# A gated delta rule with a triangular solve: a new order of steps, three elements in flight, the solve's turned blocks by transfer

## The chip, the cores and the metric

One core of one Trainium2 chip runs the program. The metric is device time in microseconds, from start to end of one launch. The core has five instruction queues that run beside each other: TensorE (PE), VectorE (DVE), ScalarE (ACT), GpSimd (POOL) and SyncE (SP, here for DMA only). Each runs its instructions in the order written and waits on semaphores where another queue's result is needed.

## The reference, cut to what matters

For each of 32 batch elements x (256 tokens x 128 features) the kernel does an attention-like layer and a small feed-forward layer, and adds both to x:

```
xn = layernorm(x)
q, k, v = silu(causal_conv4(xn @ Wq | Wk | Wv))      # 12 heads, 64 wide for q and k, 128 for v
beta = sigmoid(xn @ Wb + b_b);  g = -exp(A_log) * softplus(xn @ Wgk + dt_bias)
q, k = l2norm(q) * 64**-0.5, l2norm(k)
for each token t, each head:                         # S is 64 x 128
    S  = S * exp(g_t)
    S += k_t (outer) (v_t - k_t S) * beta_t
    o_t = q_t S
attn = (rms_norm(o) * (xn @ Wg) * sigmoid(xn @ Wg)) @ Wo
ffn  = fp4(silu(fp4(xn) @ fp4(w_gate)) * (fp4(xn) @ fp4(w_up))) @ fp4(w_down)
out  = x + attn + ffn
```

fp4(.) rounds blocks of 16 numbers to eight magnitudes. All is fp32.

## The kernel before, in words

The recurrence over tokens is done in two chunks of 128 tokens per head. Inside a chunk the products k_i.k_j with their decays form a triangular 128 x 128 matrix whose inverse is needed; there are 12 heads x 2 chunks = 24 of them per element (NU). Their 32 x 32 diagonal blocks, 4 x 24 = 96, are inverted on POOL, one block in each partition ("lanes"): SP writes the blocks from the tile UP to a DRAM tensor `to_lanes` (step LOUT, four transfers) and loads them as 96 lanes into `laneA` (LLOAD); POOL solves by columns (LANEP, 30 pairs of a product at L568 and a sum at L571, each waiting for the one before by `link`); SP stores them (STORE) and fetches them back onto the diagonals (FETCH, four transfers). The larger blocks of the inverse then come from small matmuls on PE: MY, MZ for 64 x 64 and MY2, MX, MZ2 for 128 x 128. Some of these need diagonal blocks turned; the kernel before turns them on VectorE (MT, L986, three stream transposes for each group of 8 units, read from UP, written to the tile N64).

Work on one element is written as named steps. `ORDER` is a list of (step, index, offset): in iteration `it` the step is done for element it + offset. Each engine walks the same list (`of(it)`) and emits only its own part of each step, so ORDER fixes the order in every queue. A name without r is the product on PE (QK: projection of q and k for a head pair; VP: values; QT, VT, KT, OT, HT: transposes; DD: the decays; GR: k.k and k.q; GC: cumulative gates; GP: gate; WO, YO: output; FU: feed-forward); with r it is the reader on ACT or DVE. QKt and VPt are the taps of the convolution on VectorE (L856), QKs and VPs the silu, QN and SSr the norms, CJ scalars, GRr the masked products into UP (L950), DDg POOL's input of DD (L549), LN and LN2 the layer norm (VectorE, with rstd at L538 on POOL and the load of xin by SP), XQ0 and HQ the fp4 rounding, SE and SO the pipelined slots of the recurrence over heads, SQ, OS and OG output norm and gate (rO at L577 is on POOL). PE's results go to six PSUM banks used as a ring; `ring_plan` works the uses out from ORDER.

In the kernel before all of an element's steps have offset 1 up to the first pieces of the solve and offset 0 after. The loop (`run`) does iterations -1 and 0 straight, then a hardware loop of 15 bodies with two iterations each, then the last one. LN and LN2 of the next element stand near the head of ORDER, behind three of the solve's four pieces (LANEP 0 to 2) and ahead of the last (LANEP 3, offset 0):

```
("VT", 2, 0), ("LN", 0, 1), ("LN2", 0, 1), ("VT", 5, 0), ("VTr", 2, 0), ("XN", 0, 1), ("XNr", 0, 1),
("QK", 0, 1), ("ZB", 0, 1), ("ZBr", 0, 1), ...
("QKt", 0, 1), ("QKr", 1, 1), ("ZBg", 0, 1), ("LANEP", 3, 0), ("DDg", 0, 1), ("STORE", 0, 0), ...
```

Of the kernel before, what the change touches and what calls it, by code (L numbers as in the profile page):

```python
# [11 lines left out]
P = 128  # L12
# [11 lines left out]
PIECES = 4  # L24
# [27 lines left out]
    ("VT", 2, 0), ("LN", 0, 1), ("LN2", 0, 1), ("VT", 5, 0), ("VTr", 2, 0), ("XN", 0, 1), ("XNr", 0, 1),  # L52
    ("QK", 0, 1), ("ZB", 0, 1), ("ZBr", 0, 1), ("QK", 1, 1), ("QKr", 0, 1), ("ZBe", 0, 1), ("QK", 2, 1),
    ("QKt", 0, 1), ("QKr", 1, 1), ("ZBg", 0, 1), ("LANEP", 3, 0), ("DDg", 0, 1), ("STORE", 0, 0), ("QKs", 0, 1),
    ("QK", 3, 1), ("VT", 4, 0), ("QKr", 2, 1), ("VP", 0, 1), ("QKt", 1, 1), ("QKs", 1, 1), ("QKt", 2, 1),
    ("QKr", 3, 1), ("VTr", 5, 0), ("VTr", 4, 0), ("DD", 0, 1), ("FETCH", 0, 0), ("VPr", 0, 1), ("QKs", 2, 1),
    ("QT", 0, 1), ("QTr", 0, 1), ("QKt", 3, 1), ("MT", 0, 0), ("QN", 0, 1), ("QT", 1, 1), ("QTr", 1, 1),
    ("MT", 1, 0), ("QT", 2, 1), ("DDg", 1, 1), ("DD", 1, 1), ("QTr", 2, 1), ("QKs", 3, 1), ("DDr", 0, 1),
    ("GC", 0, 1), ("MY", 0, 0), ("DDg", 2, 1), ("MYr", 0, 0), ("XQ0", 0, 1), ("QN", 1, 1), ("VP", 1, 1),
    ("GCr", 0, 1), ("QK", 4, 1), ("MZ", 0, 0), ("DDr", 1, 1), ("DD", 2, 1), ("QKr", 4, 1), ("MZr", 0, 0),  # L60
    ("DDg", 3, 1), ("DDr", 2, 1), ("MY2", 0, 0), ("MY", 1, 0), ("QKt", 4, 1), ("QT", 3, 1), ("VP", 2, 1),
    ("MYr", 1, 0), ("VPr", 1, 1), ("MY2r", 0, 0), ("VPr", 2, 1), ("QTr", 3, 1), ("MZ", 1, 0), ("MT", 2, 0),
    ("SSr", 0, 1), ("MY", 2, 0), ("MZr", 1, 0), ("DD", 3, 1), ("MYr", 2, 0), ("DDr", 3, 1), ("QN", 2, 1),
    ("MX", 1, 0), ("MZ2r", 0, 0), ("CJ", 0, 1), ("QK", 5, 1), ("SE", 3, 0), ("VPt", 1, 1), ("MY2r", 1, 0),
    ("QKs", 4, 1), ("MZ", 2, 0), ("GR", 0, 1), ("VPt", 2, 1), ("VPt", 0, 1), ("GRr", 0, 1), ("GRr", 1, 1),
    ("QKr", 5, 1), ("DDg", 4, 1), ("SE", 4, 0), ("MZr", 2, 0), ("GR", 1, 1), ("QKt", 5, 1), ("XQ0", 1, 1),
# [3 lines left out]
    ("QN", 5, 1), ("DDr", 4, 1), ("SO", 7, 0), ("GRr", 4, 1), ("DDg", 5, 1), ("SE", 7, 0), ("SSr", 2, 1),  # L70
    ("DD", 5, 1), ("GRr", 5, 1), ("DDr", 5, 1), ("XQ", 0, 1), ("GRr", 6, 1), ("GRr", 7, 1), ("SO", 8, 0),
# [3 lines left out]
    ("FU", 1, 1), ("LLOAD", 0, 1), ("FUr", 0, 1), ("MZ2r", 2, 0), ("FUm", 0, 1), ("FUr", 1, 1), ("SQ", 11, 0),  # L75
# [6 lines left out]
    ("OTr", 0, 0), ("VP", 4, 1), ("VTr", 0, 1), ("VPt", 3, 1), ("SO", 17, 0), ("VPs", 3, 1), ("OT", 1, 0),  # L82
# [35 lines left out]
def ring_plan(steps):  # L118

    uses, free, frees = {}, list(range(NRING)), {}
    count = [[0] * NRING for _ in range(3)]
    for kind, a, off in steps:
        free += frees.pop((kind, a), [])
        if kind not in RING:
            continue
        for j in range(TAKES.get(kind, 1)):
            assert free, (kind, a)  # L130
            b = free.pop(0)
            uses[kind, a, j] = (b, off, count[off][b], count[2][b])
            count[off][b] += 1
            count[2][b] += 1
            frees.setdefault(reader_of(kind, a, j), []).append(b)
    assert not frees
    return uses, count


def build(nc, x, Wq, Wk, Wv, Wg, Wo, conv_q, conv_k, conv_v, Wgk, Wb, b_b, A_log, dt_bias, gnorm,  # L140
# [13 lines left out]
    with ctx:  # L154
# [46 lines left out]
        eGR = sb("eGR", [P, 2, NU])  # L201
# [9 lines left out]
        sq = sb("sq", [P, 4, 2 * NT * 2, DK])  # L211
# [68 lines left out]
        s_xcd = sem("inverses_turned")  # L280
# [73 lines left out]
        def run(eng, iteration):  # L354

            for it in (-1, 0):
                parity[0] = it % 2
                iteration(it)
            with eng.Fori(1, NB - 2, 2) as it:
                for n in range(2):  # L360
                    parity[0] = (1 + n) % 2
                    iteration(it + n)
            parity[0] = (NB - 1) % 2
            iteration(NB - 1)
# [17 lines left out]
        def corner(a):  # L382

            return N64[:, (par() + a) % 2, :, :, :]

# [15 lines left out]
        def stage(k, lag):  # L401
# [13 lines left out]
            for way in ("to_lanes", "from_lanes"))  # L415

# [9 lines left out]
        def _(sp):  # L426
# [24 lines left out]
            def iteration(it):  # L451
                for kind, a, i in of(it):
# [21 lines left out]
                    if kind == "LLOAD":  # L474
                        sp.wait_ge(s_diag, cnt(i, 1, 1) * 16 * NBL)
                        if not zero(i):
                            hold(sp)
                            sp.wait_ge(s_lout, i * 16)
                        sp.dma_start(laneA[0:LANES, :, :].rearrange("l j i -> l (j i)"),
                                     to_lanes.rearrange("q u j i -> (q u) (j i)")).then_inc(s_lin, 16)  # L480
                    if kind == "STORE":
                        sp.wait_ge(s_solved, cnt(i, 1, 1))
                        if not zero(i):
# [4 lines left out]
                                     laneA[0:LANES, :, :].rearrange("l j i -> l (j i)")).then_inc(s_lout, 16)  # L488
                    if kind == "FETCH":
# [9 lines left out]
        def _(pool):  # L499
# [6 lines left out]
            nc.gpsimd.memset(N64[:, :, :, :, :], 0.0)  # L506
# [15 lines left out]
            chain = [0, 0, 0]  # L522

            def iteration(it):
                first_it = isinstance(it, int) and it < 0
                i0, base = (0, 0) if first_it else (it, chain[2])
                if not first_it:
# [7 lines left out]
                for kind, a, i in of(it):  # L535
# [22 lines left out]
                    if kind == "LANEP":  # L558
# [22 lines left out]
            def counted(it):  # L581
# [9 lines left out]
        def _(act):  # L591
            act.wait_ge(s_wload, 16 * 19)
            nc.scalar.activation(negA[:, :], negA[:, :], ACT.Exp).then_inc(s_seta, 1)
            chain = [0, 0, 0]

            def iteration(it):
                first_it = isinstance(it, int) and it < 0
                i0, base = (0, 0) if first_it else (it, chain[2])
                if not first_it:
# [7 lines left out]
                for kind, a, i in of(it):  # L607
# [63 lines left out]
                    if kind == "VT":  # L671
# [3 lines left out]
                        if not zero(i):  # L675
# [678 lines left out]
```

## Time and profile before

| | |
|---|---|
| median of 3 runs | 3294.02 us (3276.98, 3294.02, 3296.87) |
| the profiled execution | 3276.51 us, span 3274.8 us |
| mean granted TensorE clock | 0.937 of full |
| busy: PE, DVE, ACT, POOL | 2721.0, 2617.8, 2193.7, 1549.4 us |
| DMA | 73.30 MB, q1 9.1% of 16 engines' span |

Busy time is the union of an engine's instructions. In the rows below a bracket at the end of a timeline row is the idle time of the engine just before it and what ended it. The clock column is the share of full TensorE clock granted in the stretch. Line numbers are those of the kernel before.

### The profile page before, as it was taken

How to read it: one execution, taken by the hardware profiler on the slowest of the kernel's cores; microseconds unless marked ns; L12 is line 12 of the kernel's file. 1: busy time of each engine (PE TensorE's matmuls, PEld its weight loads, DVE VectorE, ACT ScalarE, POOL GpSimd, SP SyncE). 2: the span in 40 equal slices, each digit the busy share in tenths (PEclk: the TensorE clock that was granted, in tenths of full speed). 3: DMA queues.
4: the chain of work that ended last, by engine and by line, in shares of the span. 5: the costliest groups of instructions: out<-in, count | busy, mean ns of one | idle time of the engine just before them, and what ended most of it. 6: DMA issues, size and time to landing. Idle time of an engine off the chain costs nothing.

```text
span 3274.8 us, 84555 instructions
## 1 busy us (share of the span) xinstructions
PE 2721.0 (83%) x25330; PEld 2140.6 (65%) x25487; DVE 2617.8 (80%) x7460; ACT 2193.7 (67%) x6594; POOL 1549.4 (47%) x2386
## 2 busy tenths in 40 slices
PE   4588888788888888888888888888878888888896
PEld 2467666676666666666677666667666667666675
DVE  6688888788887878878788887878878788787882
ACT  3466766676776667767667676767767677666674
POOL 1455434554435554445554345554355544355541
PEclk8799999899999999999999999999999999999997
DMA  1110010110110100101100101101101101101100
GB/s 48 22 25 18 20 27 14 27 26 17 23 26 16 26 22 17 26 18 23 26 20 19 27 15 26 26 17 23 26 16 26 26 16 23 27 15 27 26 15 14
DMA packets 241563, 73.30 MB, mean 22 GB/s; under 512 B 207408, under 2 KB 234352, under 8 KB 241008
## 3 DMA queue, kind: packets, MB, share of 16 engines
q1 hardware_dynamic: 241008, 66.71, 9.1%
q8 instruction: 250, 4.10, 0.6%
q14 instruction: 305, 2.50, 0.3%
HBM read 37.32 MB, written 29.36 MB: 20 GB/s over the span
## 4 chain that ended last, share of the span: by engine, by line
DVE 33%; POOL 27%; issue 23%; DMA 6%; PE 6%; SPq 2%; POOLq 1%; DVEq 1%; ACT 1%; ACTq 0%
POOL laneA L571 12%; POOL laneT L568 12%; DVE KQ L856 8%; DVE UP L950 8%; DVE vc L856 4%; DVE N L986 3%; DMA laneA<-to_lanes 3%; DMA to_lanes<-UP 3%; PE ring L1127 2%; POOL rO L577 2%; SPq L473 1%; POOLq L533 1%; DVE ssr L919 1%; DVE xn L880 1%; DVE V L1005 1%
## 5 line engine op out<-in xcount | busy, mean ns | idle before, releaser
L571 POOL TENSOR_TENSOR laneA<-laneA,laneT 96x30 f32<-96x30 f32 (+14 forms) x960 | 514.7, 536 | 75.6
L568 POOL TENSOR_TENSOR laneT<-laneA 96x30 f32<-96x30 f32 (+14 forms) x960 | 488.4, 509 | 68.1 <-POOL laneA L571 0.2
L555 POOL TENSOR_TENSOR sqk<-sse,phalf 128x8 f32<-128x8 f32 x96 | 157.3, 1638 | 700.5 <-DVE sse L924 700.5
L856 DVE SCALAR_TENSOR_TENSOR KQ<-ring,ckq,KQ 128x255 f32<-128x255 f32 (+2 forms) x1152 | 462.9, 475 | 14.4 <-DVE nabs L888 7.0
L856 DVE SCALAR_TENSOR_TENSOR vc<-ring,cvv,vc 128x255 f32<-128x255 f32 (+2 forms) x1152 | 460.0, 475 | 1.2
L549 POOL TENSOR_TENSOR gm<-g,mle 128x512 f32<-128x512 f32 x192 | 197.2, 1048 | 361.8 <-DVE UP L950 270.1
L577 POOL TENSOR_TENSOR rO<-ov,mhalf 128x8 f32<-128x8 f32 x96 | 162.2, 1690 | 357.6 <-DVE ov L1016 350.4
L950 DVE SCALAR_TENSOR_TENSOR UP<-ring,cj,gm 128x256 f32<-128x256 f32 x768 | 317.2, 478 | 2.3 <-PE ring L1144 1.2
L1027 DVE SCALAR_TENSOR_TENSOR V<-V,rO,ring 128x128 f32<-128x128 f32 x768 | 214.8, 343 | 121.5 <-POOL rO L577 62.3
L758 ACT ACTIVATE junk<-V 128x128 f32<-128x128 f32 x768 | 233.8, 314 | 107.0 <-DVE V L1011 96.9
L1127 PE MATMUL ring<-xnT,wqk 128*128 128x256 f32 x768 | 268.3, 501 | 16.8 <-ACT xnT L623 15.2
L1118 PE MATMUL ring<-gm,mgt 128*128 128x512 f32 x384 | 216.7, 647 | 69.5 <-POOL gm L549 55.4
L1291 PE MATMUL bank_o<-Sb,KQ 128*128 128x128 f32 x1536 | 244.7, 282 | 2.9 <-ACT V L732 1.2
L1005 DVE SCALAR_TENSOR_TENSOR V<-bank_o,negG,V 128x128 f32<-128x128 f32 x384 | 133.6, 348 | 123.6 <-PE bank_o L1297 91.3
L1127 PEld LDWEIGHTS ring<-xnT,wqk 128*128 128x128 f32 x768 | 185.2, 255 | 64.4 <-ACT xnT L623 25.9
L1158 PE MATMUL ring<-xnT,wv 128*128 128x256 f32 x768 | 210.9, 397 | 17.0 <-DVE V L1027 10.4
L1291 PEld LDWEIGHTS bank_o<-Sb,KQ 128*128 128x128 f32 x1536 | 202.7, 192 | 30.2 <-issue 11.6
L642 ACT ACTIVATE KQ<-ring,ckq 128x256 f32<-128x256 f32 x384 | 159.3, 465 | 88.9 <-PE ring L1127 88.1
L1144 PE MATMUL ring<-KQ 64*128 64x256 f32 x768 | 198.9, 393 | 22.4 <-issue 13.7
L1145 PE MATMUL ring<-KQ 64*128 64x256 f32 x768 | 199.9, 394 | 0.0
L749 ACT ACTIVATE otb<-ring 128x512 f32<-128x512 f32 x192 | 116.2, 605 | 123.3 <-PE ring L1305 83.5
L1324 PE MATMUL ring<-wo,otb 128*128 128x128 f32 x1536 | 196.6, 277 | 0.0
(164 smaller groups left out, 7703.8 us busy)
## 6 DMA issues: line engine op xcount, KB each, us to landing
to_lanes<-UP SPq DMA_DIRECT2D x128, 96.0 KB, 2.2
laneA<-to_lanes SPq DMA_DIRECT2D x32, 384.0 KB, 3.2
from_lanes<-laneA SPq DMA_DIRECT2D x32, 384.0 KB, 3.0
UP<-from_lanes SPq DMA_DIRECT2D x128, 96.0 KB, 2.4
xin<-_attn_hidden_states_dram SPq DMA_DIRECT2D x32, 128.0 KB, 2.2
xres<-_attn_hidden_states_dram SPq DMA_DIRECT2D x32, 128.0 KB, 2.9
out_dram<-yb SPq DMA_DIRECT2D x32, 128.0 KB, 1.8
wv<-in_L_attn_Wv_dram SPq DMA_DIRECT2D x1, 768.0 KB, 5.3
```

What stands on the lines that cost most here:

```text
L568: link(nc.gpsimd.tensor_tensor(t, A[:, 0:m, j:j + 1].broadcast_to([LANES, m, n]), A[:, j:j + 1, j + 1:BLK].broadcast_to([LANES, m, n]), AL ...
L571: link(nc.gpsimd.tensor_tensor(w, w, t, ALU.add))
L577: nc.gpsimd.tensor_tensor(out=rO[:, :, uq], in0=ov[:, :, uq], in1=mhalf[:, 0:8].rearrange("p (t h) -> p t h", t=NT), op=ALU.pow).then_inc( ...
L758: ins = nc.scalar.activation(junk[:, t, :], V[:, t, h, :], ACT.Square, accum_out=ssO[:, t, h:h + 1])
L856: ins = nc.vector.scalar_tensor_tensor(acc[:, n, s:T], src[:, n * T:n * T + T - s], wt(n)[:, TAPS - 1 - s:TAPS - s], acc[:, n, s:T], ALU.m ...
L950: ins = nc.vector.scalar_tensor_tensor(UP[:, par(), NT * a + t, :, :], b[:, t * 2 * P:(t + 1) * 2 * P].rearrange("p (k n) -> p k n", k=2), ...
L1027: ins = nc.vector.scalar_tensor_tensor(v, v, rO[:, t, 4 * q + n:4 * q + n + 1], gate[:, n * P:(n + 1) * P], ALU.mult, ALU.mult)
L1118: mm(b[:, :], mgt[:, :], decay(a).rearrange("p h t n -> p (h t n)"), start=True, stop=False)
L1127: ins = mm(b[:, w * T:(w + 1) * T], wqk[:, w, a * P:(a + 1) * P], xnT[:, par(), :], start=True, stop=True)
L1145: o_done = mm(odd[:, o], KQ[krows(1), a, 0, ts], KQ[krows(1), a, :, ts], start=True, stop=True)
L1158: ins = mm(b[:, n * T:(n + 1) * T], wv[:, h * P:(h + 1) * P], xnT[:, par(), :], start=True, stop=True)
L1291: ins = mm(BO[:, w * P:(w + 1) * P], KQ[:, h // 2, w, P:2 * P], Sb[:, h % 2, :], start=True, stop=True)
```

## The change

- LN and LN2 get offset 2, behind the steps that still read the one before; `run` has iterations -2 to 3 straight, 13 loop bodies of two, and two iterations straight behind. `rv`, `ring_plan` and the chain counts are extended for that.
- The solve is cut in 8 pieces instead of 4, all with offset 1, so that the whole solve stands within one iteration, ahead of the next one's XN and DDg.
- Behind the last piece POOL copies 72 of the 96 lanes turned (row and column swapped) from laneA to a new tile laneX. SP stores it to a DRAM tensor (TSTORE) and three transfers bring the blocks into N64 (TFETCH). MT on VectorE is gone; MY waits for TFETCH, MZ for FETCH.
- The values V have two buffers (V2), N64 holds all 24 units instead of two groups, eG is written by ScalarE straight into its double buffer (two exponentials), and sq has two slots instead of four.
- ORDER is new throughout. Its head, and the steps named later:

```
("XN", 0, 1), ("XNr", 0, 1), ("QK", 0, 1), ("VPs", 4, 0), ("ZB", 0, 1), ("VT", 2, 0), ("VP", 0, 1),
("ZBr", 0, 1), ("STORE", 0, 0), ("VPs", 5, 0), ("QKr", 0, 1), ("ZBe", 0, 1), ("QK", 1, 1), ("QK", 2, 1),
("QKr", 1, 1), ("QKt", 0, 1), ("QKr", 2, 1), ("VP", 1, 1), ("VTr", 2, 0), ("QK", 3, 1), ("QK", 4, 1),
("QKr", 3, 1), ("ZBg", 0, 1), ("QKt", 1, 1), ("QKr", 4, 1), ("GC", 0, 1), ("GCr", 0, 1), ("TSTORE", 0, 0),
("QKs", 0, 1), ("VPr", 0, 1), ("DDg", 0, 1), ("QKt", 2, 1), ("QKs", 1, 1), ("QT", 0, 1), ("QKt", 3, 1),
("VT", 5, 0), ("DDg", 1, 1), ("QTr", 0, 1), ("QKs", 2, 1), ("QT", 1, 1), ("QT", 2, 1), ("QTr", 1, 1),
("VTr", 5, 0), ("QKt", 4, 1), ("VT", 4, 0), ("QKs", 3, 1), ("DDg", 2, 1), ("TFETCH", 0, 0), ("DD", 0, 1),
("VPr", 1, 1), ("VTr", 4, 0), ("QTr", 2, 1), ("VP", 2, 1), ("QN", 0, 1), ("QK", 5, 1), ("VPt", 1, 1),
("VPr", 2, 1), ("DDr", 0, 1), ("DD", 1, 1), ("DDr", 1, 1), ("VPt", 2, 1), ("DD", 2, 1), ("MY", 0, 0),
("MY", 1, 0), ("MY", 2, 0), ("MYr", 0, 0), ("FETCH", 0, 0), ("MZ", 0, 0), ("DDg", 3, 1), ("QN", 1, 1), ...
("GRr", 11, 1), ("SO", 9, 0), ..., ("LOUT", 0, 1), ..., ("LLOAD", 0, 1), ..., ("OS", 0, 0), ..., ("LN2", 0, 2), ...
("LANEP", 0, 1), ..., ("LANEP", 1, 1), ..., ("LANEP", 2, 1), ..., ("OS", 1, 0), ..., ("LANEP", 3, 1), ...
("OS", 2, 0), ("VTr", 1, 1), ("LANEP", 4, 1), ..., ("LANEP", 5, 1), ..., ("LANEP", 6, 1), ..., ("LANEP", 7, 1), ...
```

The core of the rest:

```diff
-PIECES = 4
+PIECES = 8
+TURNED = 3
...
-            for it in (-1, 0):
+            for it in range(-2, 4):
                 parity[0] = it % 2
                 iteration(it)
-            with eng.Fori(1, NB - 2, 2) as it:
+            with eng.Fori(4, NB - 3, 2) as it:
...
+                    if kind == "TSTORE":
+                        sp.wait_ge(s_turn, cnt(i, 1, 1))
...
+                        sp.dma_start(turned.rearrange("q u j i -> (q u) (j i)"),
+                                     laneX[0:TURNED * NU, :, :].rearrange("l j i -> l (j i)")).then_inc(s_tout, 16)
+                    if kind == "TFETCH":
+                        sp.wait_ge(s_tout, cnt(i, 1, 1) * 16)
...
+                        for q in range(TURNED):
+                            r = slice(BLK * q, BLK * q + BLK)
+                            sp.dma_start(N64[r, :, q % 2, :], turned[q].rearrange("u j i -> j u i")).then_inc(s_xcd, 16)
...
                         if a == PIECES - 1:
                             pool.sem_inc(s_solved, 1)
+                            if not zero(i):
+                                pool.wait_ge(s_tout, i * 16)
+                                hold(pool)
+                            nc.gpsimd.tensor_copy(laneX[0:TURNED * NU, :, :],
+                                                  laneA[0:TURNED * NU, :, :].rearrange("l j i -> l i j")).then_inc(s_turn, 1)
...
-                    if kind == "MT":
-
-                        if a == 0:
-                            dve.wait_ge(s_xc, cnt(i, 1, 1) * 16 * NBL)
...
-                        for q in range(3):
-                            r = slice(BLK * q, BLK * q + BLK)
-                            ins = nc.vector.transpose(corner(a)[r, :, q % 2, :], UP[r, par(), units(a), 0, r])
-                        ins.then_inc(s_xcd, 1)
...
                     if kind == "MY":
                         b = take("MY", a)
-                        pe.wait_ge(s_xcd, cnt(i, NG, a + 1))
+                        if a == 0:
+                            pe.wait_ge(s_xcd, cnt(i, 1, 1) * 16 * TURNED)
...
                         pe.wait_ge(read("MY", a), rv(i, "MY", a))
+                        if a == 0:
+                            pe.wait_ge(s_xc, cnt(i, 1, 1) * 16 * NBL)
```

## Rows read from the trace of the kernel before

**Rows 1.** The page, part 1: busy us (share of the span) x instructions.

```profile
PE 2721.0 (83%) x25330; PEld 2140.6 (65%) x25487; DVE 2617.8 (80%) x7460; ACT 2193.7 (67%) x6594; POOL 1549.4 (47%) x2386
```

**Rows 2.** The page, part 4: the chain that ended last, by engine.

```profile
DVE 33%; POOL 27%; issue 23%; DMA 6%; PE 6%; SPq 2%; POOLq 1%; DVEq 1%; ACT 1%; ACTq 0%
```

**Rows 3.** The timeline of SyncE, stores of the lanes: start us, us, what.

```profile
131.22 0.31 SPq L487 DMA_DIRECT2D from_lanes<-laneA  x1
...
1519.77 0.33 SPq L487 DMA_DIRECT2D from_lanes<-laneA  x1
...
1620.31 0.33 SPq L487 DMA_DIRECT2D from_lanes<-laneA  x1
...
1717.38 0.33 SPq L487 DMA_DIRECT2D from_lanes<-laneA  x1
...
3199.98 0.32 SPq L487 DMA_DIRECT2D from_lanes<-laneA  x1
```

**Rows 4.** The timeline of SyncE: LOUT of two elements.

```profile
1669.31 2.10 SPq L473 DMA_DIRECT2D to_lanes<-UP  x4
...
1766.34 2.09 SPq L473 DMA_DIRECT2D to_lanes<-UP  x4
```

**Rows 5.** The timelines of VectorE and POOL around one solve.

```profile
1665.99 3.23 DVE L950 SCALAR_TENSOR_TENSOR UP<-ring,cj,gm 128x256 f32<-128x256 f32 x8
...
1676.19 0.15 POOL L563 MEMSET laneA<- 96x32 f32 x1 [1.15 <-DMA laneA<-to_lanes]
...
1710.05 0.70 POOL L538 TENSOR_TENSOR rstd<-veps,mhalf 128x2 f32<-128x2 f32 x1 [0.45 <-DVE veps L876]
...
1716.88 0.26 POOL L571 TENSOR_TENSOR laneA<-laneA,laneT 96x30 f32<-96x30 f32 x1
```

**Rows 6.** The timeline of TensorE: VP, DD 0, QT, MY 0 and the next XN.

```profile
1623.41 1.03 PE L1158 MATMUL ring<-xnT,wv 128*128 128x256 f32 x4
1625.79 1.12 PE L1118 MATMUL ring<-gm,mgt 128*128 128x512 f32 x2 [1.35 <-POOL gm L549]
1628.04 1.99 PE L1136 MATMUL ring<-ident,KQ 128*128 128x128 f32 x12 [1.13 <-DVE KQ L856]
...
1632.33 0.69 PE L1203 MATMUL ring<-N,UP 32*32 32x32 f32 x32 [0.70 <-DVE N L986]
...
1711.95 0.69 PE L1098 MATMUL ring<-ident,xn 128*128 128x128 f32 x2 [2.78 <-DVE xn L880]
```

**Rows 7.** The waits of VectorE: in total us, times, longest us.

```profile
DVE z L885 <- PE ring L1106: 117.2, 31, 4.1
...
DVE V L1027 <- POOL rO L577: 62.3, 16, 4.3
...
DVE xn L880 <- POOL rstd L538: 44.3, 32, 17.9
```

**Rows 8.** Stretches: us; busy PE, PEld, DVE, ACT, POOL; PEclk, DMA, GB/s.

```profile
1620.30:1717.40 97.10, 84.09 (x792) 65.97 (x797) 81.02 (x233) 68.35 (x207) 48.38 (x74) 0.96 0.10 22
1618.00:1621.00 3.00, 3.00 (x11) 2.55 (x10) 1.81 (x6) 2.22 (x4) 1.66 (x6) 0.50 0.01 3
```

**Rows 9.** The groups by line: MT's transposes.

```profile
L986 DVE STREAM_TRANSPOSE N<-UP 32x256 f32<-32x256 f32 x288 | 124.1, 431 | 21.5 <-DMA UP<-from_lanes 14.0 <-PE ring L1082 4.9
```

**Rows 10.** The timeline of POOL: gm, and the widest sum of the solve.

```profile
1658.79 1.05 POOL L549 TENSOR_TENSOR gm<-g,mle 128x512 f32<-128x512 f32 x1
...
1698.71 0.65 POOL L571 TENSOR_TENSOR laneA<-laneA,laneT 96x240 f32<-96x240 f32 x1
```

**Rows 11.** The page, part 6: issues, KB each, median us to landing.

```profile
from_lanes<-laneA SPq DMA_DIRECT2D x32, 384.0 KB, 3.0
UP<-from_lanes SPq DMA_DIRECT2D x128, 96.0 KB, 2.4
```

**Rows 12.** VectorE's bq: one in the timeline, then all: ns min/median/max.

```profile
1658.83 1.04 DVE L912 TENSOR_SCALAR bq<-sse 128x8 f32<-128x8 f32 x1
...
L912 DVE TENSOR_SCALAR bq<-sse x96: 171/173/1041, 61.2 to 3147.6; 128x8 f32<-128x8 f32 x96
```

More of the change, by code:

```diff
@@ L51 @@
 ORDER = (
[L52 to L56, printed above, removed]
@@ L62 @@
[L62 to L66, printed above, removed]
[3 rows of a table removed]
@@ L91 @@
+    ("OG", 5, 0), ("WO", 3, 0), ("OTr", 4, 0), ("OT", 5, 0), ("HT", 1, 1), ("OTr", 5, 0), ("WO", 4, 0),
+    ("WO", 5, 0), ("HTr", 0, 1), ("LANEP", 7, 1), ("HTr", 1, 1), ("VPt", 5, 1), ("YOr", 0, 0),
 )
@@ L123, in ring_plan @@
     uses, free, frees = {}, list(range(NRING)), {}
-    count = [[0] * NRING for _ in range(3)]
+    spans = ((0, 2), (1, 2), (2, 2), (0, 1), (0, 0))
+    count = [[0] * len(spans) for _ in range(NRING)]
     for kind, a, off in steps:
@@ L131, in ring_plan @@
             b = free.pop(0)
-            uses[kind, a, j] = (b, off, count[off][b], count[2][b])
-            count[off][b] += 1
-            count[2][b] += 1
+            uses[kind, a, j] = (b, off, tuple(count[b]))
+            for n, (lo, hi) in enumerate(spans):
+                count[b][n] += lo <= off <= hi
             frees.setdefault(reader_of(kind, a, j), []).append(b)
@@ L312, in split, with early @@
                 hold(eng)
+        def early(i):
+            return isinstance(i, int) and i < 2
         def zero(i):
@@ L323, in rv @@
         def rv(i, kind, a, j=0):
-            b, off, alone, n = ring[kind, a, j]
+            b, off, (n, n1, n2, m1, m0) = ring[kind, a, j]
+            every, u1, u2, v1, _ = ring_uses[b]
             it = i - off
+            if isinstance(it, int) and it == -2:
+                return n2 + 1
             if isinstance(it, int) and it == -1:
-                return alone + 1
+                return u2 + n1 + 1
+            if isinstance(it, int) and it == NB - 2:
+                n = m1
             if isinstance(it, int) and it == NB - 1:
-                n = alone
-            return it * ring_uses[2][b] + (ring_uses[1][b] + n + 1)
+                return u2 + u1 + (NB - 2) * every + v1 + m0 + 1
+            return it * every + (u2 + u1 + n + 1)
         def bank(kind, a, j=0):
@@ L382, in corner @@
         def corner(a):
-            return N64[:, (par() + a) % 2, :, :, :]
+            return N64[:, units(a), :, :]
         def decay(a):
@@ L415, in build @@
             for way in ("to_lanes", "from_lanes"))
+        turned = nc.dram_tensor("turned_lanes", [TURNED, NU, BLK, BLK], F32, kind="Internal").ap()
         def units(a):
@@ L505, in _ @@
             nc.gpsimd.memset(phalf[:, :], 0.5)
-            nc.gpsimd.memset(N64[:, :, :, :, :], 0.0)
+            nc.gpsimd.memset(N64[:, :, :, :], 0.0)
             nc.gpsimd.memset(Sb[:, :, :], 0.0).then_inc(s_setp, 1)
@@ L526, in iteration @@
                 i0, base = (0, 0) if first_it else (it, chain[2])
-                if not first_it:
+                if isinstance(it, int) and it == NB - 1:
+                    i0, base = 0, 0
+                    chain[1] = chain[0] + (NB - 2) * chain[2] + chain[3]
+                elif not first_it:
                     chain[1] = chain[0]
@@ L586, in counted @@
                     chain[2] = chain[1] - chain[0]
+                if isinstance(it, int) and it == NB - 2:
+                    chain[3] = chain[1] - chain[0]
             run(pool, counted)
@@ L598, in iteration @@
                 i0, base = (0, 0) if first_it else (it, chain[2])
-                if not first_it:
+                if isinstance(it, int) and it == NB - 1:
+                    i0, base = 0, 0
+                    chain[1] = chain[0] + (NB - 2) * chain[2] + chain[3]
+                elif not first_it:
                     chain[1] = chain[0]
@@ L767, in counted @@
                     chain[2] = chain[1] - chain[0]
+                if isinstance(it, int) and it == NB - 2:
+                    chain[3] = chain[1] - chain[0]
             run(act, counted)
@@ L833, in turned_weights @@
                 dve.sem_inc(s_setd, 1)
-            chain = [0, total[0], 0]
+            chain = [0, total[0], 0, 0]
             def iteration(it):
@@ L839, in iteration @@
                 i0, base = (0, 0) if first_it else (it, chain[2])
-                if not first_it:
+                if isinstance(it, int) and it == NB - 1:
+                    i0, base = 0, 0
+                    chain[1] = chain[0] + (NB - 2) * chain[2] + chain[3]
+                elif not first_it:
                     chain[1] = chain[0]
@@ L1043, in counted @@
                     chain[2] = chain[1] - chain[0]
+                if isinstance(it, int) and it == NB - 2:
+                    chain[3] = chain[1] - chain[0]
             run(dve, counted)
```

110 lines of the change are left out of this document (57 added, 53 removed), and 35 rows, old and new, of the table ORDER.

## The prediction

> **What bounds the kernel now.** I read the page first: TensorE is busy for 83% of the span and VectorE for 80% [rows 1], so no engine is full, and the chain that ended last is spread over DVE 33%, POOL 27% and "issue" 23% [rows 2]. A chain split like that is a loop through several engines, so the next view is the one row per element that marks the end of its lane solve, SyncE's store [rows 3]. The first stands at 131.22, the last at 3199.98: 31 periods in 3068.8 us, 99.0 each, with 131.2 of filling before and 74.8 of emptying behind. Neighbouring periods differ: 1519.77 to 1620.31 is 100.5, the next 97.1. Of the 31, 14 are longer than 99.5 (mean 101.1) and 17 are not (mean 97.3), and a loop with 15 bodies of two elements has 14 jumps back: a jump costs 101.1 - 97.3 = 3.8 us.
>
> The loop inside one period is seen from one element's rows. Its last GRr (8 instructions from 1665.99 for 3.23) end at 1669.2, LOUT is issued at 1669.31, and after its transfer and LLOAD's POOL's memset starts at 1676.19: 7.0 us [rows 4, 5]. The solve then holds POOL until 1717.1 [rows 5]. But the next element's rstd stands in POOL's queue behind the third quarter, so it comes at 1710.05, TensorE's XN at 1711.95 [rows 5, 6], and from there to the next LOUT at 1766.34 it is 54.4 us [rows 4]. 1669.3 to 1766.3 is the whole period: an element can't begin before three quarters of the solve ahead of it.
>
> At this seam the engines starve. VectorE waits 117.2 us in 31 times for ZB, 44.3 for rstd, and 62.3 in 16 times for rO [rows 7]. After a jump the granted clock is 0.50 (1.2 GHz) at 1618 to 1621 though TensorE is busy all of it; over 1620.3 to 1717.4 TensorE is busy 84.09 us at mean clock 0.96, VectorE 81.02 [rows 8].
>
> **The change, part by part,** in us per element.
>
> *LN two elements ahead.* rstd, LN and LN2 no longer stand between the solve and XN; their work is the same. XN needs an LN2 done a third of a period before. The old loop is gone, and what follows it decides.
>
> *MT removed.* Nine transposes of 431 ns are 124.1 us in all, 3.9 per element, off VectorE [rows 9]; the copy of eG goes too, 0.2. GC's exponential becomes two instructions on ScalarE, busy 68.35 of 97.1 [rows 8]: nothing; if that cover went, 0.3.
>
> *Turned lanes by transfer.* POOL copies 72 lanes of 1024 elements, read across. No row shows such a copy. The nearest are gm, 512 elements in 1.05 us, and laneA, 240 in 0.65 [rows 10]: 2.0 to 2.7 ns per element, so 2.1 to 2.8. I take 2.1, since only one operand is read; ends kept are 1.0 (half of that again) and, for a stride that no row has, four times it, 8.4. TSTORE repeats STORE (0.33 of issue, 3.0 to landing), TFETCH has three transfers of FETCH's kind (issues some 0.5 apart, 2.4 to landing) [rows 3, 4, 11]: 3.3 + 4.0 = 7.3 from the copy's end to MY. FETCH now stands behind TFETCH on SyncE; its four land 2.3 later, so MZ is ready 9.6 after the copy. SyncE's LN load stands behind FETCH, with some 10 us until VectorE reads xin; XR and YOr keep their places.
>
> *Solve in eight pieces, whole before DDg.* The 60 operations are the same. 1676.19 to 1717.1 is 41; less rstd (0.70) and its wait (0.45) it is 40, with two rO in it [rows 5]. The third rO stands behind one piece less, which takes most of VectorE's waits for it away.
>
> *Values and corners doubled, sq halved.* Waits on the previous element's OT fall away; sq's two slots want each QN within two steps, which the order grants. Nothing, up to 0.5 both ways.
>
> *The order.* Three bounds on the new period follow.
> (1) Lanes through MY. Last GRr to memset 7.0, solve 40, copy 2.1, transfers 7.3: 56.4. From MY 0 (1632.33) to the last GRr's end (1669.2) is 36.9 now [rows 5, 6]. The new order has VP 1, VP 2, QK 4, QK 5 and DD 2 ahead of MY 0 instead of behind: five products of about 1.03 [rows 6] are 5.1, leaving 31.8. Sum 88.2; through FETCH and MZ, 1.9 further in the order, 88.6.
> (2) Lanes through POOL's queue. DDg 0 waits for the copy: 49.1, + 1.05 for DDg 0. From DD 0 on TensorE (1625.79) to the last GRr is 43.4 now; QK 4, VP 1, the QT of three pairs (1.99) and GC go ahead of it [rows 6], 4.4 together, leaving 39.0. Sum 89.2.
> (3) The engines. VectorE: 81.0 - 4.1 = 76.9 of work, and of its 16.1 idle us half of ZB's wait (1.9), all of rstd's (1.4) and most of rO's (1.5) go: 11.3 stay, 88.2. TensorE: 84.1 less what 1.2 GHz costs, 4% or 3.4, is 80.7, plus 8 of 13 idle us (XN's 2.78 [rows 6] and about 2 more of the seam go): 88.7.
> Bounds this close don't hide each other wholly. I add 2.5, about TensorE's waits for gm (1.35) and for MT (0.70) today [rows 6], and take 91.5. The ends are 88.5 and 97.3.
>
> *Loop form.* 13 bodies, so 12 jumps at 3.8 are 46 (14 are 53 now). Filling: element 1's XN no longer waits for element 0's solve; its first steps run beside it, some 5 us: 126. Emptying: the copy and the second transfer in place of MT, 1.3: 76.
>
> **Sum:** 31 x 91.5 = 2836.5, + 46 + 126 + 76 = 3084, against the profile's span of 3274.8 (its run took 3276.5). That is 191 less, 5.8%. The runs' median, 3294.0, is 17.5 above the profiled run, and two of three lie there; for a median the forecast is 3086 plus most of that: **3100**.
>
> **A rule weighed.** VectorE's bq has a median of 173 ns but took 1.04 us from 1658.83, beside POOL's gm from 1658.79 to 1659.84 [rows 10, 12]. The taps and the GRr around it, which read PSUM, show nothing like it. So I charge nothing for the copy's company: beside it VectorE has mostly taps. The Trainium skill, SBUF — State Buffer, "SBUF: two separate sides", calls the port pair that VectorE and GpSimd share an exclusive lock held for the whole instruction. bq's row agrees; if each copy held VectorE for its 2.1 us by that lock, the sum would be 3149 instead of 3084.
>
> **The rivals.**
> A, the forecast: the seam closes, period 88.5 to 94, jumps kept. 0.55.
> B, the overlap is whole: 88.5, and a jump half hidden since POOL solves across it: 31 x 88.5 + 23 + 126 + 76 = 2969, with the median's offset 2985. For it: TensorE's gaps are mostly at the seam. Against: three bounds at once. 0.12.
> C, the lane loop holds longer. The rO of heads 8 to 11 stands before the last four pieces; if VectorE's last O slots come late, half a solve waits for them. With bound 88.6 and such a wait of 6.4, or one of 4.3 and the 2.1 of the copy beside VectorE, the period is 95: 95 x 31 + 46 + 202 = 3193, median some 3205. For it: the bounds leave no slack. 0.16.
> D, the shift does nothing: many small waits along the engines set the period, MT's time turns into idle, and 97.3 stays: 31 x 97.3 + 46 + 202 = 3264, within 1%. Against: the seam's waits are plain in the rows. 0.08.
> E, slower: the copy across lanes is the new wait, in POOL's queue ahead of DDg 0 and of TSTORE, with nothing to cover it once the loop binds. It decides from a loop of 97.6 (no change), and slower by 1% from 98.7: bound 88.6 + 10.1, a copy of 12.2 us, 12 ns an element against the rows' 2.0 to 2.7. At 14 us the period is 100.5 and the time 31 x 100.5 + 248 = 3364. 0.09.
>
> **How the numbers follow.** About 1% is what a measurement here tells from none. Faster by over 1% is A, B and C, 0.83; within 1% is D and a sliver of E, 0.09; slower 0.08. The range 3005 to 3230 leaves out half of B's weight, D in part and E, about 0.2.
>
> **What the changed profile would show.** Stores of lanes about 91.5 apart, 95.3 at jumps. XN right behind WO, z's wait for ZB halved, rstd's gone, no stream transpose. Mean clock over 0.96 between jumps. The copy at 2.1 us, MY some 7.3 behind it. If TensorE waits over 2 us for N64's transfer or for gm, the lane loop binds (C, or E if the copy is long). If the copy is short, MY never waits and the period is still 97, then D holds and I had the wrong loop.

## The result and the profile after

| | before | after |
|---|---|---|
| median | 3285.82 us (4 runs, 3276.98 to 3296.87) | 3111.20 us (4 runs, 3109.63 to 3114.79) |
| ratio, 95% interval | | 0.9469 (0.9430 to 0.9507) |
| the profiled execution | 3276.51 us, span 3274.8 | 3109.63 us, span 3107.9 |
| mean granted TensorE clock | 0.937 | 0.931 |

The change makes the kernel 5.3% faster. The page, part 1, answers to [rows 1]:

```profile
PE 2683.1 (86%) x25361; PEld 2160.6 (70%) x25487; DVE 2498.6 (80%) x7140; ACT 2210.9 (71%) x6626; POOL 1621.8 (52%) x2418
```

VectorE has 119 us less work and stands at 80% as before, TensorE went from 83 to 86%, POOL from 47 to 52%. The time is in SyncE's timeline, where one element's round reads as in [rows 3, 4], with the two new steps between (start us, us, what):

```profile
1534.52 0.32 SPq L507 DMA_DIRECT2D from_lanes<-laneA  x1
...
1625.12 0.32 SPq L507 DMA_DIRECT2D from_lanes<-laneA  x1
1627.29 0.30 SPq L515 DMA_DIRECT2D turned_lanes<-laneX  x1
1630.66 1.46 SPq L525 DMA_DIRECT2D N<-turned_lanes  x3
1632.16 2.23 SPq L530 DMA_DIRECT2D UP<-from_lanes  x4
...
1676.18 2.11 SPq L492 DMA_DIRECT2D to_lanes<-UP  x4
...
1724.36 0.31 SPq L507 DMA_DIRECT2D from_lanes<-laneA  x1
```

1534.52 to 1625.12 is 90.6, the next 99.2. The first store stands at 133.41, the last at 3034.25: 31 periods of 93.6 on average, where they were 99.0. Every second one in the loop is long (97.8 to 101.7, 12 in all), the other 19 are 88.5 to 92.7 and 90.2 on average. The copy, from POOL's tiles (ns min/median/max):

```profile
L617 POOL COPY laneX<-laneA x32: 1890/1988/2013, 133.5 to 3034.4; 72x1024 f32<-72x1024 f32 x32
```

The waits by line (total us, times, longest us) answer to [rows 7]:

```profile
DVE z L940 <- PE ring L1152: 146.4, 31, 9.9
PE ring L1144 <- issue: 69.2, 12, 6.4
PE ring L1250 <- DMA N<-turned_lanes: 18.5, 2, 18.2
DVE V L1071 <- POOL rO L622: 5.2, 7, 1.5
DVE xn L935 <- POOL rstd L578: 0.8, 1, 0.8
```

The waits of the old seam are gone: rO from 62.3 us to 5.2, rstd from 44.3 to 0.8. MY waits for the turned lanes only twice, while the pipeline fills and empties. What grew is z's wait for ZB, in spite of the closed seam, and TensorE has a new wait in front of XN, 12 times 5.8 us, as many as there are jumps back. ("issue" means that the profile shows nothing that it waited for. The kernel before had such a wait in front of VT, 14 times 4.6 us.) The timelines of TensorE and VectorE at a jump:

```profile
1611.81 1.95 PE L1373 MATMUL ring<-wo,otb 128*128 128x128 f32 x16
1619.29 0.69 PE L1144 MATMUL ring<-ident,xn 128*128 128x128 f32 x2 [5.53 <-issue]
1620.45 2.08 PE L1173 MATMUL ring<-xnT,wqk 128*128 128x256 f32 x4 [0.47 <-ACT xnT L673]
...
1623.24 0.21 DVE L940 TENSOR_TENSOR z<-ring,zbias 128x48 f32<-128x48 f32 x1 [9.02 <-PE ring L1152]
```

And without a jump, one element earlier:

```profile
1522.51 0.38 PE L1144 MATMUL ring<-ident,xn 128*128 128x128 f32 x2
1523.36 1.13 PE L1173 MATMUL ring<-xnT,wqk 128*128 128x256 f32 x4 [0.47 <-ACT xnT L673]
...
1524.89 0.21 DVE L940 TENSOR_TENSOR z<-ring,zbias 128x48 f32<-128x48 f32 x1 [1.76 <-PE ring L1152]
```

The same two transposes take 0.69 us behind the stall and 0.38 without it, QK 0 2.08 and 1.13. The stretches (columns as in [rows 8]) are a short period, a long one, and 12 us of a jump at which TensorE stood from 1613.76 to 1619.29:

```profile
1525.00:1615.00 90.00, 79.76 (x782) 63.97 (x783) 77.98 (x222) 67.11 (x204) 49.76 (x75) 0.96 0.14 29
1615.00:1714.00 99.00, 86.73 (x796) 70.51 (x801) 77.89 (x222) 70.02 (x210) 50.06 (x76) 0.90 0.14 28
1617.00:1620.00 3.00, 0.69 (x2) 0.29 (x2) 0.00 (x0) 0.00 (x0) 2.61 (x6) 0.50 0.01 3
1620.00:1623.00 3.00, 2.55 (x8) 2.19 (x9) 0.00 (x0) 1.86 (x5) 2.53 (x7) 0.50 0.03 8
1623.00:1626.00 3.00, 3.00 (x10) 2.60 (x11) 2.35 (x7) 2.24 (x6) 2.34 (x7) 0.50 0.02 7
1626.00:1629.00 3.00, 3.00 (x14) 2.58 (x13) 2.65 (x9) 1.73 (x5) 1.96 (x2) 0.87 0.68 197
```

VectorE's work is the same in both periods; TensorE is busy 7 us longer in the long one. The clock is granted at 0.50 (1.2 GHz) for 9 us, from 1617 to 1626, of which 6.7 lie behind the stall. So a jump costs twice: TensorE stands 5.5 us, and then works at half speed.

### The profile page after: what moved, and what is told of

It reads as the page before. It is cut to its first block and busy times, and to the rows that moved or that the text cites. A ratio compares the mean times of both kernels' runs of the same rounds, so it can differ in the third digit from the quotient of the medians.

```text
span 3107.9 us, 84227 instructions
## 1 busy us (share of the span) xinstructions
PE 2683.1 (86%) x25361; PEld 2160.6 (70%) x25487; DVE 2498.6 (80%) x7140; ACT 2210.9 (71%) x6626; POOL 1621.8 (52%) x2418
## 5 line engine op out<-in xcount | busy, mean ns | idle before, releaser
L1190 PE MATMUL ring<-KQ 64*128 64x256 f32 x768 | 238.2, 453 | 54.8 <-DVE KQ L911 41.3
L773 ACT ACTIVATE eps<-bank_e 128x128 f32<-128x128 f32 x384 | 105.8, 276 | 225.8 <-PE bank_e L1326 184.6
L1049 DVE SCALAR_TENSOR_TENSOR V<-bank_o,negG,V 128x128 f32<-128x128 f32 x384 | 133.2, 347 | 146.6 <-PE bank_o L1346 95.3
L1173 PE MATMUL ring<-xnT,wqk 128*128 128x256 f32 x768 | 216.1, 414 | 26.6 <-ACT xnT L673 15.6
L1191 PE MATMUL ring<-KQ 64*128 64x256 f32 x768 | 239.0, 455 | 0.0
L1219 PE MATMUL ring<-wg,xnT 128*128 128x512 f32 x384 | 202.9, 610 | 28.3 <-DVE vc L911 18.7
L1190 PEld LDWEIGHTS ring<-KQ 64*128 64x128 f32 x768 | 156.4, 219 | 98.6 <-ACT sq L703 23.9
L578 POOL TENSOR_TENSOR rstd<-veps,mhalf 128x2 f32<-128x2 f32 x32 | 22.5, 703 | 386.1 <-DVE veps L931 386.1
L1182 PE MATMUL ring<-ident,KQ 128*128 128x128 f32 x768 | 143.9, 338 | 87.5 <-ACT KQ L698 78.6
```

Source lines behind the costliest of these rows:

```text
L1173: ins = mm(b[:, w * T:(w + 1) * T], wqk[:, w, a * P:(a + 1) * P], xnT[:, par(), :], start=True, stop=True)
L1190: e_done = mm(even[:, o], KQ[krows(0), a, 0, ts], KQ[krows(0), a, :, ts], start=True, stop=True)
L1191: o_done = mm(odd[:, o], KQ[krows(1), a, 0, ts], KQ[krows(1), a, :, ts], start=True, stop=True)
L1219: mm(b[:, :], xnT[:, par(), o:o + P], wg[:, q * 512:(q + 1) * 512], start=True, stop=True)\
```

## The experiments

**The changed kernel written out straight.** All 32 iterations without a loop.

```diff
-            with eng.Fori(4, NB - 3, 2) as it:
-                ...
+            for it in range(-2, NB):
+                parity[0] = it % 2
+                iteration(it)
```

> The new kernel with all 32 iterations written out, no hardware loop. In its trace a period with a jump back is about 98.5 us, one without 90.2, so 12 jumps would cost 8.3 each. Theory J (the jump itself costs it: all queues but POOL's stand still until code comes, and TensorE then starts at 1.2 GHz): periods of 90 throughout, about 3110 - 12 x 8.3 = 3010 us. Rival K (it is alternation of the two halves of the body, not the jump, or straight code is fed no faster): nothing or under 30 us, 3085 to 3110.

Measured 3003.92 us, ratio 0.9148 (0.9126 to 0.9169). Stores from 132.06 to 2927.97: 90.2 per element, none above 93.2. The 12 jumps of the loop cost 107.3 us, **8.9 each**, not 3.8. VectorE's wait for ZB, which the prediction saw halved, is halved only here: 58.5 us against the 119.1 of the kernel before written out straight (the next run).

```profile
DVE z L933 <- PE ring L1145: 58.5, 31, 4.0
```


**The kernel before written out straight** (the same edit).

> The kernel before with all 32 iterations written out. By its own periods (101.1 with a jump, 97.3 without) 14 jumps at 3.8 us cost 53: 3277 - 53 = 3224 us. If a jump's true cost is 8 us there too, hidden differently in the periods, 3277 - 112 = 3165 us.

Measured 3232.10 us, ratio 0.9847 (0.9812 to 0.9883): 51.8 us for 14 jumps, 3.7 each, periods of 97.5 on average. The price read from the stores of before was right for the kernel before. It doesn't carry over to the new one. The wait for ZB:

```profile
DVE z L879 <- PE ring L1100: 119.1, 31, 4.1
```

**The jump at another place.** The steps in the same endless order, but the body begins behind SQ 11, in the middle of the recurrence.

```diff
-ORDER = (("XN", 0, 1), ..., ("SQ", 11, 0), ("FU", 1, 1), ..., ("YOr", 0, 0))
+ORDER = (("FU", 1, 1), ..., ("YOr", 0, 0), ("XN", 0, 2), ..., ("SQ", 11, 1))
```

> The changed kernel (3111.2 us) with the same steps in the same endless order, but the loop body begins 165 steps later, behind SQ 11: the jump back stands in the middle of the recurrence, where POOL waits for its lanes anyway, instead of ahead of XN. Again 12 jumps. Straight it would be 3004 us; 12 jumps at 8.9 made 3111. Theory M, what a jump costs is what of a fixed stall of some 5 us and the clock behind it isn't covered by a wait that stood there before: another place has another cost, here 4 to 8 us, 3050 to 3100. Rival N, a jump costs 8 to 9 us wherever it stands (fetching the code again for five queues): 3100 to 3120.

Measured 3065.58 us, ratio 0.9346 (0.9319 to 0.9372): (3065.6 - 3003.9) / 12 = 5.1 us per jump. TensorE at a jump:

```profile
1655.85 2.71 PE L1468 MATMUL ring<-wgu,xqT 128*128 128x352 f32 x4 [3.35 <-issue]
```

Its waits of this kind are 38.6 us in 12 times, 3.2 each, against 5.8 in front of XN, and VectorE's wait for ZB is down from 146.4 us to 55.5 in all. Rival N falls: the cost depends on where the jump stands. Theory M had the time, but not its premise of a fixed stall: here TensorE stands 3.2 us and the clock is at 0.50 for 6 us (1655 to 1661), in front of XN 5.5 and 9. So the place changes the stall as well as what covers it. How much of the cost is clock and how much is the stall on the other engines was not measured apart.

**The copy three times.** POOL does the turned copy three times before it is released.

```diff
+                            for again in range(3):
+                                link(nc.gpsimd.tensor_copy(laneX[...], laneA[...].rearrange("l j i -> l i j")))
+                            pool.sem_inc(s_turn, 1)
```

> The new kernel with the turned copy done three times on POOL, 4.0 us more in front of DDg 0 and TSTORE. If the lane loop binds (bounds 1 and 2 of the prediction), all of it shows: 31 x 4 = 124, 3235 us. If the engines bind (bound 3) and the lanes have slack, at most the part beyond the slack shows: 3110 to 3150 us.

Measured 3205.66 us, ratio 0.9758 (0.9732 to 0.9785), between the two expectations. POOL is busy 54.3 to 54.7 us of a period instead of 50. Between jumps the stores stand 94.5 apart, 4.3 more; at jumps 100.2, 1.2 more. Its waits:

```profile
PE ring L1167 <- POOL gm L589: 58.9, 19, 13.7
```

DD 0 now waits for gm 58.9 us, where it was 9.2 in the changed kernel. A longer copy costs all of itself between jumps and is mostly hidden at one.

**No turned copy.**

```diff
+                            if zero(i):
                                 nc.gpsimd.tensor_copy(laneX[...], ...).then_inc(s_turn, 1)
+                            else:
+                                pool.sem_inc(s_turn, 1)
```

> The changed kernel (3111.2 us) without POOL's turned copy from the second element on; TSTORE and TFETCH stay, so N64 gets the first element's turned lanes (that part of the result is left out). The loop of the lanes becomes 2.0 us shorter for DDg 0, and for TSTORE, TFETCH and FETCH behind it. Theory J, the lane loop sets the period and POOL's 4 us more cost 4.3 because of that: the period falls from 90.2 to 88.5 to 89.3, 3060 to 3085 us. Rival K, the engines' own work sets 90.2 and the three copies only went past a small slack: the period stays within 0.4, 3098 to 3115 us.

Measured 3113.06 us, ratio 0.9479 (0.9451 to 0.9508), against 0.9469 with the copy; periods 90.3 and 98.7. POOL's work fell from 1621.8 to 1560.6 us and nothing came of it. Theory J falls, and K's time came: the lane loop alone doesn't set the 90.2, though 4.0 us more on it cost 4.3.

**MT on VectorE again**, without copy, TSTORE and TFETCH, the new order kept.

```diff
+    ... ("VPt", 1, 1), ("MT", 0, 0), ..., ("VPt", 2, 1), ("MT", 1, 0), ("MT", 2, 0), ...
-    ("TSTORE", 0, 0), ("TFETCH", 0, 0)
```

> The new kernel with the blocks turned on VectorE again (nine transposes of 0.43 us per element, MT 0 to 2 between the steps VPt 1 and MY 0), without the turned copy, its store and its three transfers; order otherwise as in the new kernel. If VectorE's work is on the path, 3.9 us per element come back: 31 x 3.9 = 121, 3230 us. If TensorE sets the pace and the new order is what gained, under 1 us per element: 3110 to 3140 us.

Measured 3226.04 us, ratio 0.9824 (0.9797 to 0.9852), 115 us over the changed kernel. MY's waits for N are in the trace:

```profile
PE ring L1487 <- DVE N L1268: 84.4, 54, 18.3
```

From this alone one would say that MY waits for VectorE's transposes. The next run takes that wait away.

**Idle transposes.** The same nine transposes at the same places read a weight and write a dead tile; copy and transfers stay.

```diff
+                    if kind == "MT":
+                        for q in range(3):
+                            ins = nc.vector.transpose(laneX[LANES:P, GU * q:GU * q + GU, :], wqk[LANES:P, 0, ...])
+                        link(ins)
```

> The changed kernel (3111.2 us) with nine stream transposes per element put back on VectorE at the same places as when MT was back (3226.0 us), but reading a weight tile and writing a dead one, so that nobody waits for them; the copy and the transfers stay. VectorE gets 3.9 to 4.3 us more work per element. Theory L, VectorE's work is on the path and that is what MT's return cost: period about 94.5 to 95.5, 3220 to 3260 us. Rival P, MT's return cost what it did because MY waited for it: here 3111 to 3140 us.

Measured 3227.33 us, ratio 0.9831 (0.9805 to 0.9857): the same as with MT in earnest. The page:

```profile
PE 2735.8 (85%) x25361; PEld 2211.5 (69%) x25487; DVE 2610.8 (81%) x7428; ACT 2217.6 (69%) x6626; POOL 1623.3 (50%) x2418
```

VectorE is busy 112 us longer and the kernel takes 116 us longer. TensorE's products GR now wait more for KQ, which VectorE writes, here and then in the changed kernel:

```profile
PE ring L1431 <- DVE KQ L1147: 95.6, 32, 4.4
...
PE ring L1190 <- DVE KQ L911: 41.3, 30, 4.4
```

Theory L holds: work added to VectorE's queue costs its whole length, though VectorE is busy for only 81% of the span. MT's wait in the last run was no cause of its own. One part is not taken apart: the mean clock fell from 0.931 to 0.908 and TensorE is busy 53 us longer, so some of the 116 us may be TensorE at half speed behind its longer waits.

**Three value readers on ScalarE**, in the straight kernel.

```diff
-        VT_DVE = (1,)
+        VT_DVE = ()
```

> The changed kernel written out straight (3003.9 us), with VTr 1, 3 and 5 on ScalarE like the other three: VectorE's queue loses three operations of 0.69 us per element (2.1 us), ScalarE gets three times four of 0.38 (4.6 us) on top of about 67 of 90. VectorE's 3.9 us more cost 116 us (3.7 per period). Theory L, VectorE's work sets the period in both directions: 90.2 falls to 88.2 to 89, 2940 to 2970 us. Rival T, VectorE only just binds and TensorE (some 84 of 90 us busy) or the lane loop (no slack shown over 2 us) hold 90: 2990 to 3010. Above 3020, ScalarE's 4.6 us in front of other readers would be the new wait.

Measured 2999.18 us (2993.72 to 3007.79), ratio 0.9121 (0.9094 to 0.9148), not to be told from the straight kernel's 0.9148. The page:

```profile
PE 2656.5 (88%) x25487; PEld 2139.4 (71%) x25487; DVE 2442.3 (81%) x7044; ACT 2305.6 (77%) x7010; POOL 1616.9 (54%) x2418
```

VectorE lost 50 us of work (1.6 per element), the mean period is 90.3. T's time came: more work on VectorE costs in full, less of it, moved to ScalarE, brings nothing. T's reason, another bound at the same 90, is not shown by it, for ScalarE's new work may have its part in the waits:

```profile
DVE vc L904 <- ACT vc L706: 56.9, 42, 12.0
```

It was 20.9 us in 12 times in the straight kernel, 36 us less. So most of the 50 us may have been turned into this wait; the run doesn't separate the two.

**VP 0, 2 and 4 twice**, in the straight kernel.

```diff
-                        for n in range(2):
+                        for n in (0, 1, 0, 1) if a % 2 == 0 else (0, 1):
```

> The changed kernel written out straight (3003.9 us), with the products VP 0, 2 and 4 done twice into the same bank (same result): TensorE gets 3 x 0.87 to 1.03 = 2.6 to 3.1 us more work per element, VectorE nothing. Theory U, TensorE's work is on the path like VectorE's: period about 93, 3085 to 3100 us. Rival W, TensorE has idle time at these places and VectorE alone sets the period: 3004 to 3025 us.

Measured 3029.59 us, ratio 0.9226 (0.9198 to 0.9255), 25.7 us more, 0.8 per element. VP's group rose from 203.4 to 288.7 us:

```profile
L1197 PE MATMUL ring<-xnT,wv 128*128 128x256 f32 x1152 | 288.7, 388 | 3.7 <-DVE Kt L1007 3.7
```

That is 2.7 us of work per element, of which 0.8 reached the end. The mean clock was 0.954, where the straight kernel had 0.939, and TensorE's whole busy time rose by only 55 us. The result lies between U and W, 5 us above W's end: at these places most of TensorE's added work costs nothing. What part of the rest the clock gave back is open.

**The norms one element ahead**, in the new order.

```diff
-    ("LN", 0, 2) ... ("LN2", 0, 2)
+    ("LN", 0, 1), ("LN2", 0, 1), ("XN", 0, 1), ...
```

> The new kernel with LN and LN2 at offset 1 again, at the head of the order as before, so that rstd stands in POOL's queue behind the whole solve and the turned copy. If the loop through rstd was what bound the kernel before, the period becomes last GRr to memset 7, solve 40, copy 2, rstd, LN2 2, and XN to the last GRr some 50: 101 and more, 3350 to 3450 us, slower than the kernel before. If that loop was not what bound, a few us per element at most: under 3200 us.

Measured 3531.49 us, ratio 1.0748 (1.0720 to 1.0777), above the 3350 to 3450 that the loop was expected to give. Periods of 105.5 to 111, long and short ones no longer alternate. The waits:

```profile
PE ring L1377 <- DVE xn L1168: 485.9, 31, 32.6
DVE xn L1168 <- POOL rstd L811: 302.6, 32, 29.0
```

XN stands 15.7 us per element behind rstd, which now waits in POOL's queue for the whole solve. The loop that the prediction read from the trace of before exists, and with the whole solve and the copy ahead of rstd it is longer. No period shows the jump any more, which fits a jump that is hidden in this wait; a straight form was not run.

**The old order with the norms two elements ahead**, MT on VectorE, four pieces of the solve across the seam, sq's two slots as in the change.

```diff
-    ("LN", 0, 1), ("LN2", 0, 1)
+    ... ("LN", 0, 2), ("DD", 3, 1), ... ("HQ", 0, 1), ("LN2", 0, 2), ...
```

> The new kernel's code (offset 2, double values, 13 loop bodies) with the old order of steps, the solve in four pieces across the seam and the turning on VectorE; only LN stands ahead of DD 3 and LN2 behind HQ 0, two elements ahead. If the seam's loop through rstd was most of the loss, the period without a jump falls from 97.3 to about 92 or 93 although VectorE keeps its 3.9 us of transposes: 3120 to 3170 us. If the order and the freed VectorE made the gain, it stays near 96: 3230 to 3280 us.

Measured 3321.96 us, ratio 1.0110 (1.0071 to 1.0149): 1.1% slower than before, and above both expectations. The waits name a cause that has nothing to do with the seam:

```profile
ACT sq L927 <- DVE ssr L1197: 136.6, 64, 3.7
```

**The same with four slots for the squares.**

```diff
-        sq = sb("sq", [P, 2, 2 * NT * 2, DK])
+        sq = sb("sq", [P, 4, 2 * NT * 2, DK])
```

> As old_order_norm_two_ahead (3322.0 us: the old order with the norms two elements ahead, the code of the change with MT on VectorE), but with four slots for the squares as in the kernel before, so that ScalarE's square waits for no sum (it waited 136.6 us in 64 times). Theory Q, the two slots were what ate the gain of the opened seam: period about 95.5 between jumps, 3170 to 3220 us. Rival R, the old order itself leaves nothing to gain there, since its solve still crosses the seam and DDg stands behind the last piece: 3280 to 3320 us.

Measured 3248.86 us, ratio 0.9898 (0.9873 to 0.9923). The two slots had cost 73 us in the old order (in the new one ScalarE doesn't wait for them). The stores stand 97.7 and 100.1 apart by turns, which looks as if nothing were gained between jumps. But here a jump's delay is spread over two stores. LOUT, whose row stands before the solve, shows it whole (one period without a jump, one with it), and the stall is TensorE's:

```profile
1547.37 2.09 SPq L721 DMA_DIRECT2D to_lanes<-UP  x4
...
1642.47 2.10 SPq L721 DMA_DIRECT2D to_lanes<-UP  x4
...
1745.01 2.10 SPq L721 DMA_DIRECT2D to_lanes<-UP  x4
...
PE ring L1445 <- issue: 70.2, 12, 6.2
```

By LOUT the periods without a jump are 95.3 (from the second on) and the 12 with one 102.5, where the kernel before has 96.6 and 101.7 by the same rows. So the opened seam does give something in the old order, 1.4 us per element by LOUT, and 2.2 by the first five stores, ahead of any jump (95.3 against the straight 97.5). The jump takes much of it back: 7.3 us each instead of 5.1 by LOUT, with a stall of 5.9 instead of 4.6. Theory Q had the period (about 95.5) and missed that the jump grows dearer; R falls in its reason, that the old order leaves nothing to gain. A straight form of this kernel was not run. Its waits:

```profile
DVE z L1163 <- PE ring L1385: 190.0, 31, 11.0
PEld ring L1397 <- POOL gm L817: 63.5, 26, 3.0
PE ring L1397 <- POOL gm L817: 46.1, 45, 15.7
```

rstd is out of the way, and DD waits for gm instead, which POOL does behind the last piece.

## Why the prediction was right

The forecast of 3100 is 0.4% below the 3111.2. The sum was 3084 against a span of 3107.9; that it came so near is luck in part, because two terms were wrong in opposite directions. Luck helped a second time: some 14 us were added for the distance between the median and the profiled run, which was 17.5 with the three runs of then, is 9.3 with the fourth, and is 1.6 in the changed kernel.

| term | predicted | measured | difference |
|---|---|---|---|
| 31 periods without jump | 91.5 each, 2836.5 | 90.2 each, 2796 (straight kernel) | -40 |
| 12 jumps | 3.8 each, 46 | 8.7 each, 105 (rest of the 2900.8 between first and last store) | +59 |
| filling | 126 | 133.4 | +7 |
| emptying | 76 | 73.7 | -2 |

*The period.* The bounds of 88.2 to 89.2 with 2.5 on top came out 1.3 too high. That bounds so close don't hide each other was right, and the runs show it from three sides: 3.5 us more on VectorE's queue cost 3.7, two copies more on POOL's path (4.0 us and their waits) 4.3 between jumps, and 1.6 less on VectorE or one copy less on POOL brought nothing. Of the bounds, the one through MY had slack: between jumps MY 0 starts at 1546.07, 9.5 behind the copy's end at 1536.6, where the transfers were to take 7.3. The one through DDg was close: DD 0 doesn't wait in the loop, but with 4.0 us more on POOL it waits 3.1 each time. The margin of 2.5 was a guess at what such a tie costs; 90.2 is 1.0 above the highest bound.

*The jump.* This is the step that failed: "12 jumps at 3.8 are 46". The 3.8 was taken as the price of the loop form, but it was the price beside the seam's waits. In the kernel before, TensorE stood 4.65 us at a jump and the XN behind it waited 0.65 for xn instead of 2.78 [rows 6]: its timeline there reads

```profile
1612.25 1.96 PE L1166 MATMUL ring<-ident,vc 128*128 128x128 f32 x8 [4.65 <-issue]
1614.86 0.69 PE L1098 MATMUL ring<-ident,xn 128*128 128x128 f32 x2 [0.65 <-DVE xn L880]
```

So 2.1 us of the stall lay in a wait that was there anyway. The change takes this wait away, and the jump is uncovered. That accounts for 2.1 of the 5.2 us between 3.7 and 8.9, and the longer stall (5.8 instead of 4.6) for 1.2 more; the rest is open. The clock is not what differs: in the kernel before it stood at 0.50 from 1609 to 1621, for longer than the 9 us of the changed one; how much of it lay beside waits was not measured. Five prices fit this: none to be seen where XN waits 15.7 us, 3.7 in the kernel before, 5.1 in the middle of the recurrence, 7.3 in the old order with the seam opened (by LOUT, where the kernel before has 5.1), 8.9 in front of an XN that is ready. The prediction considered that a jump might become cheaper (rival B) and not that closing the seam makes it dearer.

*The filling.* The 5 us of overlap were an error of reasoning: up to its own store, element 0 has nothing to gain from element 1's running beside it. LOUT came 2.5 us later than before (89.50), and the solve took 36.4 us where it had taken 35.8.

*The copy and the transfers.* 2.1 predicted, 1.99 measured. From its end to the last TFETCH issue it is 5.0 us, and MY never waits in the steady loop. Rivals C and E fall: no period between jumps reaches 95. B falls too (90.2 instead of 88.5, and a jump that is dearer), and so does D, whose 97.3 didn't stay.

*MT.* 3.9 off VectorE was the right size and worth its whole length: putting it back costs 3.7 per element, by VectorE's queue and not by MY's wait. Of the 7.3 between the straight kernel before (97.5) and the straight kernel after (90.2) that leaves 3.6. If the parts add up, the opened seam has 1.4 to 2.2 of it, by what it gave in the old order, and the new order the rest. Which steps of the new order bring it was not taken apart.

*The solve.* 1585.27 to 1624.9 is 39.6, 40 predicted; rO's waits went as forecast.

*The clock* did not rise over 0.96 between jumps. There is another sparse stretch at 1531 to 1534, where TensorE is busy 1.15 of 3 us while it waits for KQ, and the clock is 0.50 to 0.60 for the 6 us behind it.

*The rule weighed.* VectorE's sum of two SBUF operands, sp (ns min/median/max), stood beside idle time of POOL before and beside the solve now:

```profile
L949 DVE SCALAR_TENSOR_TENSOR sp<-z,lz x32: 171/360/934, 39.2 to 2938.9; 128x24 f32<-128x24 f32 x32
```

It was 171/175/180 before. At the jump above one starts at 1626.47 and takes 0.69, to 1627.16; the copy ends at 1627.11. The Trainium skill, SBUF — State Buffer, "SBUF: two separate sides", names for this lock a VectorE instruction with two SBUF inputs beside a GpSimd instruction that reads SBUF, and has the later one wait for the whole of the other. sp is such an instruction, and the trace agrees. But the 18 taps, which read one input from PSUM, take 7.10 us at 1572.19 in the straight kernel, where the copy starts beside them at 1576.84, and 7.10 at 1628.17 in the changed kernel, where it is over. So the charge of 2.1 us per element, for a copy that stops whatever VectorE runs beside it (3149), falls; it would need instructions like sp for the copy's whole length.

## What to carry to other kernels

A cost that is read from a trace is what the waits around it leave of it. When a change takes a wait away, price again everything that happens at the same place, the jump of the loop and the clock behind a stall above all. And read a period from more than one row: a delay that falls between two stores looks smaller in each. Where several loops come within a few per cent of each other, test each by making it longer: the one that costs in full may still give nothing when it is made shorter. A short probe with dead work on an engine tells its time from its waits, which the list of waits can't.

Where a program of that length can be had, write the loop out: the straight form of the changed kernel is the fastest that was found with a clear difference, 3003.92 us, 3.4% below the changed one.

## What the hardware showed that was not expected

- A jump back of a program on five queues cost 3.7 to 8.9 us by its place and by the waits there, and TensorE stood 3.2, 4.6, 5.8 or 5.9 us at it (means of four kernels) for "issue". That this is the fetching of code is a guess that no run here shows.
- At a stall of 5.5 us the clock went to 0.50 (1.2 GHz) for 9 us, and stayed there though TensorE was busy for 5.5 of the last 6 of them.
- POOL's copy of 72 x 1024 elements with row and column swapped took 1.99 us, 1.9 ns per element, less than the 2.7 of its widest sum (0.65 for 240).
